# A gated-delta layer with 32 experts on one core: input in groups, other places, other loads and another order of the work

## The chip, the core and the metric

The kernel runs on one core of a Trainium2 chip. The core has five engines that run side by side and meet only at semaphores: TensorE (PE: matmuls and transposes, into eight banks of PSUM), VectorE (DVE), ScalarE (ACT), GpSimd (POOL) and SyncE (SP), whose queue issues nearly all DMAs here. The metric is the device time of one execution in microseconds (us). Each engine works through its own instructions in the order in which the program lists them; an instruction that waits holds up all behind it. A DMA is issued by a queue and lands later.

## What is computed

For x of 2048 tokens by 256 features, all in fp32:

```python
x = x + attn(layernorm(x))
x = x + ffn(layernorm(x))

# attn
qkv = silu(causal_conv4(x @ W_qkv.T))         # 2048 channels
z, beta = x @ W_z.T, sigmoid(x @ W_b.T)
g = -exp(A_log) * softplus(x @ W_a.T + dt_bias)
q, k = l2norm(q) * 64 ** -0.5, l2norm(k)      # 8 heads of 64, each for 2 of 16 value heads
# per token t and head: S = S*exp(g_t); S += k_t (v_t - k_t S)^T * beta_t; o_t = q_t S
y = norm_weight * rmsnorm(o) * silu(z)
return y @ W_out.T

# ffn
h = rmsnorm(x) * norm_w
w, ids = top_k(softmax(h @ router_w.T), 4)    # 32 experts, w normed to sum 1
routed = sum_k w_k * ((silu(h @ w1_g) * (h @ w1_u)) @ w2)[ids_k]
return x + routed + (silu(h @ sg) * (h @ su)) @ sd
```

## The kernel before

**Work.** The recurrence is done by chunks of 64 tokens: 32 chunks, four in a pair of blocks; a block has 128 tokens, so there are 16 blocks and 8 pairs `p`. For each pair a *front* does what does not need the state: `proj p s i` (PE, eight slices `s` of two tiles), `mul` (ACT) and `tap` (DVE), `sum` (POOL) and `silu` for the convolution, `ss`, `ssq`, `rpow` for the norms, `kt`, `kn`, `kb`, `ke` to bring k into shape, `scan p c` for the decay between tokens of chunk `c`, `kk` and `nt` for the products within a chunk, and then the inverse of a unit triangular matrix for 32 heads and chunks at once: `lg`, `lx`, 31 steps of elimination `el` on DVE (lines 829 and 832), `xt` (its second transpose is line 896), `ta`, `pm`, `pe`, `tm`, `tc`. A *chain* goes through the chunks with the state: `kqs`, `ktb`, `v`, `ks`, `qs`, `r`, `sd`, `u`, `ue`, `ku`, `au`, `su`, `oe`; `su n` adds to the state and ends chunk `n`. A *tail* finishes each block: `osq`, `nin`, `npow`, `yn`, `yt`, `yg`, `op` (output product), `x2`, `xn`, `hh` (norms), `ht`, `htb`, `rt` (router), `mx`, `ex`, `tk`, `rank`, `slot` (top 4 and the places of the rows), and `send`, four indirect DMAs of POOL that write the rows to DRAM, sorted by expert.

**Experts.** After that come 16 shared items (one for each block) and 95 tiles of 128 sorted rows. Step `n` of `experts` does the up product of item `n`, the transposes of item `n-1` and the down product of item `n-2`. The rows of a tile go to DRAM (`picked`), and at the end each block's four rows are loaded, summed and stored.

**Order.** One list, `SCHEDULE`, is walked by every engine; each takes from it the stages that it has a part in. It is made by sorting the stages of all pairs by a planned time, `PAIR * p + t`, with `t` from tables of numbers that are the same for every pair. `banks_in_turn` gives the short-lived results one of four PSUM banks in turn.

**SP's part.** SP walks the same list. `dload p` loads the decay tables of the four chunks of pair `p + 1`, two DMAs for each chunk, each after `nt` has freed its place; `scan` waits for them. `ebload n` loads the decay of chunk `n + 1`, `xload p` the columns of pair `p + 1`, `xin` the rows of a block. `base b` stores `base` and, after a wait for `htb`, the transposed rows of block `b`. `blanks b` writes 4.2 MB of blank rows to DRAM (`blank_ranks`), which `send` needs two blocks later. `early` loads the first half of the expert weights (6.7 MB, with the two shared experts) over the front's places after the last `tc`; after the last chunk SP loads the other half and the results of 15 blocks.

**Opening.** Before the list, the whole x is normed in a few large operations, transposed, multiplied for the gates, and the tables are made and stored. The first `proj` follows.

Of the kernel before, what the change touches and what calls it, by code (L numbers as in the profile page):

```python
# [9 lines left out]
ALU = mybir.AluOpType  # L10
X = mybir.AxisListType.X

P = 128
# [28 lines left out]
TURNS = 4  # L42

# [3 lines left out]
PAIR = 95.20  # L47
FRONT = [(-89.34, "nd", 0), (-88.1, "nd", 1), (-60.93, "proj", 0, 0), (-59.88, "proj", 0, 1), (-59.83, "xload"), (-59.78, "blank"),
    (-58.65, "mul", 0, 0), (-57.71, "mul", 0, 1), (-56.59, "tap", 0), (-54.5, "proj", 1, 0), (-54.49, "sum", 0), (-53.45, "proj", 1, 1),
    (-53.16, "silu", 0), (-51.88, "mul", 1, 0), (-51.7, "proj", 2, 0), (-50.94, "mul", 1, 1), (-50.65, "proj", 2, 1),  # L50
    (-49.42, "mul", 2, 0), (-49.38, "tap", 1), (-48.48, "mul", 2, 1), (-47.3, "sum", 1), (-45.97, "silu", 1), (-44.51, "proj", 3, 0),
    (-43.46, "proj", 3, 1), (-42.53, "tap", 2), (-42.23, "mul", 3, 0), (-41.29, "mul", 3, 1), (-40.45, "sum", 2), (-38.31, "ss", 0),
    (-36.67, "tap", 3), (-36.13, "silu", 2), (-34.59, "sum", 3), (-33.91, "ssq", 0), (-33.44, "rpow", 0), (-33.26, "silu", 3),
    (-31.8, "ss", 1), (-29.8, "kt", 0), (-28.65, "kt", 1), (-28.47, "kn", 0), (-27.5, "kb", 0), (-26.27, "ke", 0), (-25.35, "kn", 1),
    (-20.49, "ssq", 1), (-20.11, "kb", 1), (-20.11, "rpow", 1), (-18.88, "ke", 1), (-18.61, "proj", 4, 0), (-17.56, "proj", 4, 1),
    (-16.33, "mul", 4, 0), (-15.39, "mul", 4, 1), (-10.62, "tap", 4), (-8.72, "scan", 0), (-7.49, "sum", 4), (-5.84, "silu", 4),
    (-5.29, "nd", 2), (-4.84, "proj", 5, 0), (-3.79, "proj", 5, 1), (-3.16, "scan", 1), (-2.56, "mul", 5, 0), (-1.74, "nd", 3),
    (-1.62, "mul", 5, 1), (-1.29, "kk", 0), (0.09, "tap", 5), (2.69, "nt", 0), (4.44, "scan", 2), (4.47, "sum", 5), (5.68, "scan", 3),
    (5.8, "silu", 5), (5.87, "proj", 6, 0), (6.92, "proj", 6, 1), (8.84, "mul", 6, 0), (9.78, "mul", 6, 1), (10.9, "tap", 6),
# [30 lines left out]
def schedule():  # L90
# [7 lines left out]
    for _, item in sorted(timed, key=lambda e: e[0]):  # L98
        out.append(item)
        if item[1] == NB - 1 and item[0] in ("x2", "xn", "rt", "ex", "tk", "rank", "slot", "send") and step < NB - 3:  # L100
            out.append(("experts", step))
            step += 1
# [1276 lines left out]
```

## Time and profile before

| | |
|---|---|
| three runs, median (lowest to highest) | 1275.51 us (1269.92 to 1276.7) |
| profiled execution: its own time | 1274.97 us |
| its span, first to last instruction | 1273.2 us |
| mean granted TensorE clock | 0.839 of full |
| busy: PE, DVE, POOL, ACT | 978.7, 822.4, 557.4, 530.0 us |
| moved by DMA | 165.67 MB, mean 130 GB/s |

The span is that of the profiled execution; the few us between it and the execution's time lie around the first and the last instruction. A busy time is the sum of an engine's instructions over the span; which engine sets the pace in a stage must be read from that stage. The granted clock is a mean; PE's instructions have two lengths, one for each of its two clocks.

### The profile page before, as it was taken

The page shows a single profiled execution, that of the slowest core. Times are in us where ns is not written, and L with a number is a line of the kernel's source. Part 1 is how long each engine was busy: PE and PEld are TensorE (multiplying, and loading weights), DVE is VectorE, ACT ScalarE, POOL GpSimd, SP SyncE. Part 2 cuts the span into 40 slices and gives each one's busy share as a digit, 9 for nine tenths or more (in the row PEclk, how much of TensorE's full clock was granted, in tenths as well). Part 3 has the DMA queues.
Part 4 walks back from the last instruction along what each step waited for, and adds up shares of the span by engine and source line. Part 5 has one row for each costly group of instructions (what it writes and reads, how often), then busy time and mean ns, then how long its engine had stood idle before and what let it go on. Part 6 is the DMA issues. An engine that isn't in the chain of part 4 may idle for free.

```text
span 1273.2 us, 32965 instructions
## 1 busy us (share of the span) xinstructions
PE 978.7 (77%) x12871; PEld 819.2 (64%) x12871; DVE 822.4 (65%) x1859; ACT 530.0 (42%) x1042; POOL 557.4 (44%) x507
## 2 busy tenths in 40 slices
PE   0685599789889879978977986886785799989940
PEld 0573577667778677767867776775674467767730
DVE  5227867877896986888689698779333343333345
ACT  1343365256355544625635453451332224434410
POOL 2034454465364555546445554543342105545530
PEclk9768689769779976977987897697697999999975
DMA  5373302055326706714640670661796814444346
GB/s 213 75 193 95 96 11 60 23 149 149 89 63 155 182 23 164 190 39 114 160 124 21 169 200 23 160 169 34 178 350 250 276 42 126 128 123 130 110 144 204
DMA packets 182359, 165.67 MB, mean 130 GB/s; under 512 B 75699, under 2 KB 174908, under 8 KB 181312
## 3 DMA queue, kind: packets, MB, share of 16 engines
q1 hardware_dynamic: 172272, 144.60, 41.3%
q0 software_dynamic: 7632, 16.87, 4.2%
q8 instruction: 106, 1.74, 0.6%
q10 hardware_dynamic: 2304, 2.10, 0.5%
q14 instruction: 45, 0.37, 0.1%
HBM read 66.03 MB, written 101.55 MB: 132 GB/s over the span
## 4 chain that ended last, share of the span: by engine, by line
PE 38%; DVE 33%; issue 11%; POOL 7%; DMA 7%; ACT 3%; SPq 1%; DVEq 0%; POOLq 0%; ACTq 0%
DVE arena L829 6%; DVE arena L832 6%; PE ps L1305 6%; PE ps L1093 4%; POOL nrm L503 3%; DVE arena L845 3%; PE ps L1156 3%; PE ps L1238 3%; PE ps L1102 2%; PE ps L1328 2%; DMA out<-work 2%; POOL slotted L580 2%; DVE work L920 2%; DMA work<-htd 2%; PE ps L1296 2%
## 5 line engine op out<-in xcount | busy, mean ns | idle before, releaser
L1093 PE MATMUL ps<-work,arena 128*128 128x259 f32 x512 | 164.0, 475 | 18.8 <-DVE arena L845 16.3
L531 POOL TENSOR_TENSOR arena<-arena 128x512 f32<-128x512 f32 x64 | 84.7, 1324 | 141.6 <-DVE arena L845 141.5
L1093 PEld LDWEIGHTS ps<-work,arena 128*128 128x128 f32 x512 | 116.3, 238 | 45.6 <-DVE arena L845 18.8
L591 POOL DMA_INDIRECT picked<-work x95 | 93.4, 983 | 113.0 <-DVE work L1026 64.2
L845 DVE SCALAR_TENSOR_TENSOR arena<-ps,cw,arena 128x256 f32<-128x256 f32 x256 | 107.1, 475 | 55.3 <-ACT arena L640 55.2
L1016 DVE TENSOR_TENSOR work<-work,ps 128x128 f32<-128x128 f32 (+1 forms) x111 | 34.0, 307 | 139.7 <-ACT work L746 113.2
L832 DVE TENSOR_TENSOR arena<-arena 128x31 f32<-128x31 f32 (+15 forms) x248 | 117.8, 475 | 8.5
L829 DVE TENSOR_TENSOR arena<-arena 128x31 f32<-128x31 f32 (+15 forms) x248 | 104.1, 420 | 7.5 <-POOL arena L511 1.3
L1305 PE MATMUL ps<-arena,work 128*128 x380 | 102.0, 391 | 7.1 <-issue 6.2
L646 ACT ACTIVATE arena<-arena 128x512 f32<-128x512 f32 x64 | 40.3, 629 | 157.6 <-POOL arena L531 157.6
L580 POOL DMA_INDIRECT slotted<-hr,slots x64 | 65.1, 1016 | 79.8 <-DVE slots L983 65.2
L1173 PE MATMUL ps<-work 64*64 64x64 f32 x1024 | 46.1, 253 | 54.6 <-DVE work L901 54.6
L746 ACT ACTIVATE work<-ps 128x128 f32<-128x128 f32 (+1 forms) x111 | 32.5, 292 | 119.7 <-PE ps L1305 56.0
L1173 PEld LDWEIGHTS ps<-work 64*64 64x64 f32 x1024 | 42.1, 165 | 57.8 <-issue 57.7
L1305 PEld LDWEIGHTS ps<-arena,work 128*128 128x128 f32 x380 | 65.3, 191 | 19.7 <-issue 14.2
L524 POOL TENSOR_TENSOR work<-work,nbeta 128x512 f32<-128x512 f32 x32 | 43.9, 1383 | 69.0 <-DVE ndb L810 50.5
L553 POOL TENSOR_TENSOR work<-arena,work 128x512 f32<-128x512 f32 x64 | 73.5, 1168 | 0.0
L1238 PE MATMUL ps<-work 128*128 128x256 f32 x256 | 66.7, 419 | 8.6 <-DVE work L926 7.4
L639 ACT ACTIVATE arena<-ps,cw 128x256 f32<-128x256 f32 x128 | 60.6, 474 | 23.9 <-PE ps L1093 16.8
L1238 PEld LDWEIGHTS ps<-work 128*128 128x128 f32 x256 | 54.2, 214 | 20.5 <-DVE work L926 10.4
L503 POOL TENSOR_TENSOR small<-small,mhalf 128x1 f32<-128x1 f32 x32 | 18.4, 576 | 98.6 <-DVE small L944 59.3
L1222 PE MATMUL ps<-work 128*128 128x256 f32 x256 | 61.0, 387 | 0.3 <-ACT work L715 0.2
(223 smaller groups left out, 2328.2 us busy)
## 6 DMA issues: line engine op xcount, KB each, us to landing
slotted<-blank SPq DMA_DIRECT2D x17, 4128.0 KB, 20.1
arena<-in_w SPq DMA_DIRECT2D x2, 6528.0 KB, 18.6
work<-slotted SPq DMA_DIRECT2D x95, 129.0 KB
arena<-tab SPq DMA_DIRECT2D x64, 128.0 KB, 3.4
work<-tab SPq DMA_DIRECT2D x64, 128.0 KB, 3.3
arena<-picked SPq DMA_DIRECT2D x16, 512.0 KB, 4.8
work<-xtd SPq DMA_DIRECT2D x8, 259.0 KB, 10.5
arena<-in_x SPq DMA_DIRECT2D x1, 2048.0 KB, 8.5
```

The lines of the kernel that those rows point to most:

```text
L531: g.tensor_tensor(ca[:, f % 2, :, :], ca[:, f % 2, :, :], conv_to(p, s_), ALU.add).then_inc(S["sum_out"], 1)
L553: g.tensor_tensor(kqs[:, n % 2, kind, :, :].rearrange("p (kt r) t -> p kt r t", r=2), kqn[:, p % 2, kind, :, lo:lo + C].unsqueeze(2).broad ...
L580: g.indirect_dma_start(out=slotted, out_offset=bass.IndirectOffsetOnAxis(ap=slots[:, k:k + 1], axis=0), in_=hr[:, k, :], in_offset=None).t ...
L591: g.indirect_dma_start(out=picked, out_offset=bass.IndirectOffsetOnAxis(ap=to, axis=0), in_=yrow[:, j % SLOTS, :], in_offset=None, bounds_ ...
L829: v.tensor_tensor(t, nl[:, j + 1:H, j:j + 1].broadcast_to([P, rows, cols]), tl[:, j:j + 1, 0:cols].broadcast_to([P, rows, cols]), ALU.mult ...
L832: v.tensor_tensor(tl[:, j + 1:H, 0:cols], tl[:, j + 1:H, 0:cols], t, ALU.add).then_inc(S["el"], 1)
L845: v.scalar_tensor_tensor(out=acc_, in0=bank_of("proj", p, s_, i)[:, k:k + W2], scalar=cw[:, u, k:k + 1], in1=acc_, op0=ALU.mult, op1=ALU.a ...
L1093: ins = mm(to[:, 0:WX], wqkv[:, k, m:m + P], xt2[:, p % 3, k, :], start=k == 0, stop=k == KD - 1)
L1173: ins = mm(KS[half(hp), DH * h:DH * h + DH], kqs[half(hp), n % 2, 0, h, :], state[half(hp), h, :], start=False, stop=h == KR - 1)
L1222: ins = mm(to[:, W2 * j:W2 * j + W2], wz[:, d, m:m + P], xt2[:, p % 3, d, TAPS - 1:TAPS - 1 + W2], start=d == 0, stop=d == KD - 1)
L1238: ins = mm(W3[:, 0:DIM], ygt[:, u, :], wo[:, u, :], start=u == 0, stop=u == UT - 1)
L1305: ins = mm(up_[:, 0:2 * I], ht[:, j % 2, k, :], arena[:, bass.ds(at_ + 2 * I * k, 2 * I)], start=k == 0, stop=k == KD - 1)
```

## The change

- **x in groups.** x is loaded in three groups of 2, 6 and 8 blocks, with the weights of the projections between the first and the second. Each group is normed by itself: `bn_stats` and `bn_aggr` on DVE, the small steps for 1/sqrt, and one scaled copy for each block on ACT, in place. The first transposed columns are copied straight into the first pair's place as well, and the first four projections are done at once; the gate products and the tables are cut into steps (`gate 0` to `gate 3`, `tables`) that stand in the list among the first pair's stages.
- **Decay loads per chunk.** `dload p c` loads the table of chunk `c` of pair `p` itself, and stands in the list by itself; `scan p c` is done during pair `p - 1`.
- **New order.** New tables of planned times: one for pairs 0 to 5, one for pair 6, one for pair 7. A few items are put behind what they need (`HELD`).
- **Late loads.** `late` stands in the list behind the last of `base 13` and `ebload 30`. It waits for the end of the chain, loads the results of 12 blocks and then the second part of the expert weights. `early` keeps its place behind the last `tc`. The results of the other four blocks are loaded after the last `base`.
- **Shared experts in the last tails.** Up to 12 of their steps stand behind stages of the last two blocks, once the chain and `slot 13` have gone by.
- **Final sums.** Each block has its own place for its four rows, is summed in place and stored from there; eight loads may be in flight, and the sums no longer wait for stores.
- PE's waits move to where the data is needed, and `sd` also waits for `ks`.

SP's items of one pair (from the last `xt` of pair 3 on), by the old list and by the new one, without those in which SP has nothing to do:

```text
before: ebload 14, blanks 4, xin 5, base 5, ebload 15, dload 4 (pair 5, all four chunks), blanks 5, xload 5
after:  ebload 14, xin 5, dload 5 0, base 5, dload 5 1, ebload 15, dload 5 2, blanks 5, dload 5 3, xload 5
```

DVE's items from the transposes of pair 3 to the next `lx`, by the new list:

```text
xt 3, tap 4 4, x2 5, tap 4 5, xn 5, nt 4 0, nt 4 1, hh 5, scan 5 0, scan 5 1, tap 4 6, mx 5, su 12, tk 5,
nt 4 2, slot 5, su 13, scan 5 2, nt 4 3, nin 6, tap 4 7, scan 5 3, yn 6, lx 4
```

PE's: `pm 3, kk 4 0, kk 4 1, tm 3, proj 4 6, u 12, ht 5, z 3 0, rt 5, ku 12, au 12, kk 4 2, ks 13, ...`. In the last pair SP has: `xin 13, base 13, late, early, blanks 13, xin 14, base 14, blanks 14, base 15`.

The core of the diff:

```diff
+GROUPS = ((0, 2), (2, NB // 2), (NB // 2, NB)) if NB > 4 else ((0, 2), (2, NB))
+SOON = max(NB - 4, 1)
-PAIR = 95.20
+PAIR = 97.66
+STEADY = {
...
+    "dload": [(-77.6, 0), (-74.8, 1), (-59.4, 2), (-53.3, 3)],
+    "scan": [(-74.7, 0), (-71.9, 1), (-56.4, 2), (-49.4, 3)],
...
+    "kk": [(16.9, 0), (17.9, 1), (33.2, 2), (40.9, 3)],
+    "nt": [(18.1, 0), (19.8, 1), (36.3, 2), (42.5, 3)],
...
+    "blanks": [(190.7, 0), (236.2, 1)],
+}
+def opening():
+    out = [("norm", 0), ("turnx", 0)] + [("proj", 0, s, i) for s in range(2) for i in range(2)]
+    for g in range(1, len(GROUPS)):
+        out += [("norm", g), ("turnx", g)]
+        if g == 1:
+            out += [("mul", 0, s, i) for s in range(2) for i in range(2)]
+    return out + [(name, 0, s) for s in range(2) for name in ("tap", "sum", "silu")] + [("gate", 0)]
+GATES = [(("tap", 0, 2), [("gate", 1)]),
+         (("tap", 0, 3), [("gate", 2), ("gate", 3), ("tables", 0)] + [("dload", 0, c) for c in range(4)] + [("ebload", -1)]),
...
+HELD = {item: cause for c in range(4) for item, cause in (
+    (("dload", 1, c), ("nt", 0, c)), (("scan", 1, c), ("dload", 1, c)), (("nd", 1, c), ("scan", 1, c - 2))) if cause[2] >= 0}
...
+        if item in ready:
+            ready.remove(item)
+            if not ready:
+                out.append(("late", 0))
+        if item == ("tc", NP - 1):
+            out.append(("early", 0))
+        if not before and item[0] in FILL and item[1] >= NB - 2 and step < SOON:
...
-                if name == "dload" and ix[0] + 1 < NP:
-                    for n in range(4 * (ix[0] + 1), 4 * (ix[0] + 1) + 4):
-                        wait(sp, S["at_out"], n - 3)
+                if name == "dload":
+                    p, c = ix
+                    n = 4 * p + c
+                    wait(sp, S["at_out"], n - 3)
...
-                if name == "oe" and ix[0] == NC - 1:
+                if name == "late":
                     sp.wait_ge(S["au_mm"], NC)
                     sp.wait_ge(S["s_out"], NC)
+                    load_results(0, 0, SOON)
                     load_experts(1)
-                    load_results(0, 0, NB - 1)
...
+            def norm(g):
+                lo, hi = GROUPS[g]
+                n = hi - lo
+                shift, var, rstd, t0, t1 = (small[:, k, lo:hi] for k in range(5))
...
+                dve.wait_ge(s_x0[g], 16)
+                for k in range(n):
+                    ins = v.bn_stats(stats[:, k, :], xall[:, lo + k, :])
+                done(ins)
+                for k in range(n):
+                    ins = v.bn_aggr(both[:, k, :], stats[:, k, :])
+                done(ins)
...
-                wait(dve, s_o[b % 2], 16 * (b // 2))
-                v.tensor_tensor(frow[:, b % 2, :], two[:, 0, :], acc[:, b, :], ALU.add).then_inc(S["fin_out"], 1)
+                v.tensor_tensor(four[:, 0, :], four[:, 0, :], acc[:, b, :], ALU.add).then_inc(S["fin_out"], 1)
```

## Rows read from the trace of the kernel before

**Rows 1.** The page, part 4: the chain that ended last, by engine.

```profile
PE 38%; DVE 33%; issue 11%; POOL 7%; DMA 7%; ACT 3%; SPq 1%; DVEq 0%; POOLq 0%; ACTq 0%
```

**Rows 2.** Windows by stage: length; busy of PE, PEld, DVE, ACT, POOL; clock; DMA share; GB/s.

```profile
469.00:577.30 108.30, 92.94 (x1451) 80.56 (x1450) 87.40 (x195) 54.35 (x92) 56.61 (x46) 0.82 0.47 119
792.00:889.40 97.40, 74.14 (x1148) 64.13 (x1148) 77.66 (x175) 39.31 (x59) 42.76 (x38) 0.79 0.45 119
889.40:967.50 78.10, 59.93 (x1044) 52.38 (x1044) 30.94 (x88) 28.29 (x41) 28.28 (x25) 0.82 0.73 223
967.50:1042.50 75.00, 56.64 (x198) 34.65 (x199) 27.86 (x100) 15.79 (x39) 11.88 (x11) 0.86 0.69 234
1227.70:1273.20 45.50, 0.00 (x0) 0.00 (x0) 23.32 (x48) 0.00 (x0) 0.00 (x0) 0.50 0.73 231
```

**Rows 3.** Waits of DVE in one pair: total, times, longest; first and last of nine.

```profile
DVE arena L845 <- ACT arena L640: 4.2, 2, 3.3
...
DVE arena L885 <- issue: 0.6, 1, 0.6
```

**Rows 4.** Timeline of the opening, DVE and PE: start, us, what, idle before.

```profile
10.11 4.42 DVE L779 TENSOR_REDUCE small<-arena 128x16 f32<-128x4096 f32 x1 [10.11 <-DMA arena<-in_a_log]
...
41.56 5.77 PE L1056 MATMUL ps<-arena 128*64 128x16 f32 x191 [0.79 <-ACT arena L608]
49.24 3.17 PE L1056 MATMUL ps<-arena 128*64 128x16 f32 x65 [1.91 <-issue]
...
63.43 1.20 PE L1093 MATMUL ps<-work,arena 128*128 128x259 f32 x2 [0.95 <-ACT arena L624]
```

**Rows 5.** Timeline of ACT and PE in the stretch after the transposes, of two pairs.

```profile
579.18 2.07 ACT L677 ACTIVATE work<-arena,kbm 128x1024 f32<-128x1024 f32 x1 [1.64 <-DVE arena L896]
581.26 3.95 ACT L680 ACTIVATE work<-arena 32x1024 f32<-32x1024 f32 x2
...
490.46 1.41 PE L1156 MATMUL ps<-arena 32*32 32x32 f32 x43
...
492.88 2.58 PE L1156 MATMUL ps<-arena 32*32 32x32 f32 x84 [0.49 <-issue]
```

**Rows 6.** SP's issues in a pair; landings: L364, L383 there; L383, L394, L388 in all.

```profile
523.51 0.62 SPq L364 DMA_DIRECT2D slotted<-blank  x1
527.73 8.17 SPq L383 DMA_DIRECT2D work<-xtd  x1
...
DMA to landing us min/median/max: 20.5/20.5/20.5
...
DMA to landing us min/median/max: 17.4/17.4/17.4
...
DMA to landing us min/median/max: 4.0/16.5/18.1
...
DMA to landing us min/median/max: 3.0/3.3/5.0
...
DMA to landing us min/median/max: 2.9/3.4/4.4
```

**Rows 7.** SP's issues of the two parts of the expert weights.

```profile
916.12 0.35 SPq L425 DMA_DIRECT2D arena<-in_w  x1
...
967.50 0.33 SPq L425 DMA_DIRECT2D arena<-in_w  x1
```

**Rows 8.** Timeline of PE: the first shared expert, and two steps of later ones.

```profile
991.77 5.40 PE L1296 MATMUL ps<-arena,work 128*128 128x512 f32 x8 [5.06 <-DMA work<-htd]
...
1033.70 1.88 PE L1296 MATMUL ps<-arena,work 128*128 128x512 f32 x4
...
1036.50 1.88 PE L1296 MATMUL ps<-arena,work 128*128 128x512 f32 x4
```

**Rows 9.** Timeline of the final sums: their loads, and DVE's first.

```profile
1227.74 35.13 SPq L450 DMA_DIRECT2D arena<-picked  x16
...
1231.65 0.69 DVE L1035 TENSOR_TENSOR work<-arena 128x512 f32<-128x512 f32 x1 [7.90 <-DMA arena<-picked]
```

More of the change, by code:

```diff
@@ new lines @@
+ENDING = [END_0, END_1]
+PER_CHUNK = ("kqs", "ebload", "ktb", "v", "ks", "qs", "r", "sd", "u", "up", "ue", "ku", "su", "au", "oe")
+PER_BLOCK = ("osq", "nin", "npow", "yn", "yt", "yg", "op", "x2", "xin", "lnp", "xn", "rmp", "hh", "base", "hr", "ht", "htb", "rt", "mx", "ex",
+             "tk", "rank", "slot", "send", "blanks")
+FILL = ("nin", "yn", "op", "x2", "xn", "hh", "rt", "mx", "tk", "rank", "slot")
+def opening():
[5 more added lines that the diff above has]
+    return out + [(name, 0, s) for s in range(2) for name in ("tap", "sum", "silu")] + [("gate", 0)]
@@ L90, in schedule @@
 def schedule():
[L91 removed]
+    timed = []
     for p in range(NP):
[L93 to L100 removed]
+        table = STEADY if p < NP - len(ENDING) else ENDING[p - NP]
+        for name, times in table.items():
+            for t, *ix in times:
+                if name in PER_CHUNK:
+                    ix[0] += 4 * p
+                elif name in PER_BLOCK:
+                    ix[0] += 2 * p
+                else:
+                    ix = [p, *ix]
+                timed.append((PAIR * p + t, (name, *ix)))
@@ new lines, in schedule @@
+    out, step, before, ready = [], 0, {("oe", NC - 1), ("su", NC - 1), ("slot", NB - 3)}, {("base", NB - 3), ("ebload", NC - 2)}
+    planned = [item for _, item in sorted(timed, key=lambda e: e[0])]
+    head = opening()
+    moved, gates = set(head).union(*(then for _, then in GATES)), list(GATES)
+    first = head + [item for item in planned if item not in moved]
+    for item, cause in HELD.items():
+        if item in first and first.index(item) < first.index(cause):
+            first.remove(item)
+            first.insert(first.index(cause) + 1, item)
@@ L101, in schedule @@
+    for item in first:
+        out.append(item)
+        while gates and gates[0][0] in out:
+            out += gates.pop(0)[1]
+        before.discard(item)
+        if item in ready:
[5 more added lines that the diff above has]
+        if not before and item[0] in FILL and item[1] >= NB - 2 and step < SOON:
             out.append(("experts", step))
@@ L141, in banks_in_turn @@
             taken += 1
-    return out
-TURN = banks_in_turn()
+    return out, last
+TURN, LAST = banks_in_turn()
 class Chain:
@@ L628, in stage @@
+            def stage(name, *ix):
+                if name == "norm":
+                    norm(*ix)
+                if name == "turnx":
+                    transposed(*ix)
+                if name == "gate":
+                    gate(*ix)
                 if name == "mul":
@@ L1179, in stage @@
                     wait(pe, S["o_out"], n)
+                    wait(pe, S["s_out"], n)
                     for h in range(KR):
```

458 lines of the change are left out of this document (306 added, 152 removed), and 110 rows, old and new, of tables (CHAIN, END_0, END_1, FRONT).

## The prediction

> **What bounds the kernel now.** The page comes first: no engine is full, and the chain that ended last changes hands between PE (38%) and DVE (33%) [rows 1]. Such a share says nothing of a stage, so the span is cut at the eight transposes of line 896, one for each pair of blocks, and at the ends of the chain of chunks, of the shared experts and of the tiles [rows 2]. The first elimination starts at 123.2 us. Then come pairs of about 107.6 us each; in the one shown DVE is busy 87.4 of 108.3 us and PE 92.9. The last pair but one takes 97.4 us, the stage to the end of the chain 78.1 us, the shared experts with the last tail 75.0 us, and the final sums 45.5 us.
>
> The waits of DVE in that pair are short: nine groups, 4.2 us the largest, 17.8 us in all [rows 3]. So 90.5 us of the pair are DVE's own work and the gaps between its instructions, and each wait added in its queue lengthens the pair, unless another shrinks. None of the nine is for a load: this is what I expect to change.
>
> **The opening.** Before, DVE starts when 2 MB of x and the small inputs are in, at 10.1 us, and the transposes at 34.6; the gate products take from 41.6 to 52.4, and the first projection starts at 63.4 [rows 4]. After, the first 256 KB should be in at about 4 us (an eighth of the load that is in at 10.1 us). Two blocks need two statistics of the kind that `x2` takes (0.4 us each), the two aggregations and 14 small steps of about 0.2, so 4.2 us; the scaled copies, four transposes and two copies 3 us: first projection at about 11 us, not 63.4. The other two groups keep DVE until about 28 us and the last transposed columns leave at about 34. There PE does the gate products, 10.9 us, to 45. Slices 2 and 3 and the gate steps, with the queues waiting on each other, run to 58. The blanking of 4.2 MB, issued at about 44, now stands ahead of the decay table on SP's queue; as such a write takes about 20 us [rows 6], the table is stored at 64, its four loads issue in 5.4 us and land at 73, and the scans end at 75. Slices 4 to 7 took 28 us from there before; they keep this length, since the four scans that leave them make room for four new ones with short waits for loads of 3.4 us [rows 6]. First elimination: 103 us. **-20 us**, between -25 (the waits for pair 1's loads are covered) and -12 (each costs 4 us in full). The removed work (two passes of 4.4 us over x on DVE, ACT's square, the two stores of zeros) is in this difference.
>
> **The pairs.** The work is the same; the order and the loads are not. SP is in order, and two of its items stand in the way of the decay loads, on which DVE's scans wait.
>
> First, `dload q 1` stands behind `base`, which waits until `htb` of the same block is out. From the end of the transposes `xt` to that `htb`: `ta` 6.0 us, `pe` 1.1, `tm` 4.9 (490.5 to 495.4) [rows 5], `tc` 2.4, `u` 1.1, `ht` and `htb` 0.8, together 16.3 (`pe`, `tc`, `u`, `ht` and `htb` by their lengths in the same stretch); then 0.4 for the store's issue, 0.6 for the first half's and 3.4 to the landing of the second: 20.8 us. DVE's own work over that stretch is two `tap` (3.3), `x2` (1.3), `xn` (0.8), two `nt` (3.4), `hh` (1.9) and one scan (1.3), 12.0 us. New wait, that of the first scan included: about 9 us. At least 5, if the matmuls and `tc` run side by side; 10 at most. Queued behind that scan are `tap` 6, `su` and `tk`, and PE's `ks` waits for `su`.
>
> Second, `dload q 3` stands right behind `blanks`, a write of 4.2 MB. The trace has this very arrangement with another load: the write issued at 523.5 took 20.5 us, and the load of xt issued at 527.7 was held 8.2 us in issue and landed 17.4 us after it began, at 545.1, one us after the write; a decay load with nothing in front lands in 3.4 [rows 6]. In the new order `blanks` issues 1.3 us after the third `nt` of the pair, so the fourth load lands some 23 us after that `nt`. DVE has until then `slot` (1.8), `su` (0.7), the third scan (1.3), the fourth `nt` (1.7), `nin` (1.8) and `tap` 7 (1.6): 8.9 us. New wait: 14 us, the third scan's included; 12 if the write takes 18 us, 16 if 22. Behind the fourth scan stand `yn`, `lx` and the whole elimination of the next pair.
>
> The Trainium skill (DMA: Bandwidth & Descriptors, "Anatomy of one DMA") fits a DMA of its GpSimd path as 2.0 us plus its bytes at 436 GB/s, which gives 11.7 us for this write. By the 20.5 us of the row the new wait is 14 us, by the page about 5, and the whole forecast would be 1264 us. The row has the very write, so the sum goes by it.
>
> So a pair has 90.5 us of work, 24 us of new waits and what is left of the old ones. While DVE is held, the other engines catch up, and the old waits (for `op`, `ss`, `kt`, `yt`, `ex`) should fall from 17.8 to about 5: 119.5 us, 11 to 12 more than now. If the old waits vanish and the first stall is the small one, it is 6 more; if 10 us of them stay, 16. The loads of pairs 3 to 7 stand so, five stretches between transposes: **+56 us**, between +30 and +80. Pair 2's loads have neither item ahead of them and cost nothing new. In the stretch of 97.4 us there are no decay loads any more, and the four scans have gone an interval earlier: **-5 us**, between 0 and -9.
>
> **The last pair.** After the last transposes the new order has only `x2` to `slot` of block 13 ahead, where the old one had block 13's norm and products too, and the four chunks follow each other at about 10 us. From `xt`: `pm` 3.9, two `z` 4.0, `tm` 4, `z` and `tc` 3, `u`/`ku`/`su` of chunk 28 at 18, `su` 29 at 26, `su` 30 at 37 (it stands behind `yn` 14), `su` 31 at 50 to 54. With the 1.9 us of the transpose the stage is 55 us, not 78.1: **-23 us**, between -14 and -28.
>
> But `late` stands ahead of `early` in SP's queue, and waits for the end of the chain. Before, the first 6.7 MB of expert weights were issued at 916.1, and only the second part and the results at 967.5 [rows 7]; the results landed 24.2 us later, 8.65 MB at 357 GB/s, and PE started at 991.8 [rows 8]. After, the results of 12 blocks (3.1 MB) and both parts of the weights, the one that the shared experts need last, go out then: 16.5 MB, 46 us at that rate. PE's first shared expert waits for it, and PE's queue holds behind it `ht` and `rt` of block 14 and all that is left of block 15. From there: 16 experts of 2.8 us (44.8), 2.6 for the slow first, 8.2 of tails on PE, and 7.5 between `rt` 15 and `rank` 15, which no expert covers now. 109 us instead of 75.0: **+34 us**, between +24 (the load at 400 GB/s, the tail covered) and +38.
>
> **The tiles** keep their order and loads: 0. **The final sums** no longer wait for the stores of two blocks before. The stretch moves 10.5 MB in 45.5 us with the DMA engines busy 0.73 of it [rows 2]; full, that is 33 us, while DVE needs 16 x 1.55 = 25, which is hidden; with 3.8 us until the first block is there [rows 9], 37 us. **-8 us**, between -3 and -12.
>
> **Sum.** -20 + 56 - 5 - 23 + 34 - 8 = +34. The profiled execution took 1275.0 us (span 1273.2), the median of the runs 1275.5, so the base is the same: 1309 us. A measurement of this kernel can tell about 0.5%, 6.4 us, from no change.
>
> **Rivals.** (a) *The fourth load does not wait for the blanking.* A later load's packets may pass, or the blanking may be over sooner. For it: no load of `ebload` took more than 5.0 us to land, though a write is in flight for 20 of every 50 us. Against: of the seven xt loads, of which five stand close behind a write, the median is 16.5 us and the longest 18.1 [rows 6]. The fourth scan's wait falls from 14 to about 3 and 55 us go: 1254 us, faster. It decides as soon as that load lands within 12 us of the third `nt`. Chance 0.11. (b) *The new order fits better than I read it.* All old waits vanish, the `base` stall is the small one, +6 a pair: 1282 us, and with the opening or the weights at their good ends, within the noise. Chance 0.14. (c) *Nothing is caught up.* 10 us of old waits stay, +16 a pair: 1333 us. Chance 0.13. (d) *The weights arrive in time*: if SP's three loads share the engines and the shared experts start at 25 us after the chain, 21 us less: 1288 us. Against it is that the results behind 6.7 MB came last before. Chance 0.07. (e) *The forecast*, its own range 1288 to 1326: 0.55.
>
> **Numbers.** Faster: (a) and a little of (b), 0.13. Within 0.5%: the good ends of (b), 0.08. Slower: 0.79. Range for 8 in 10: 1268 to 1338, which leaves out most of (a) and the far end of (c).
>
> **What would show it.** In the changed kernel's profile: the first projection at 11 us, the first elimination at 103; transposes `xt` some 119 us apart from the second to the sixth interval; DVE's scan, which waits for nothing now, with waits on the decay load of about 9 and 12 us in each pair; PE idle some 46 us before the first shared expert, on the weights; out stores with no DVE wait on them. I am wrong if the scans' waits are a few us, or if the transposes stay 107 us apart with the waits elsewhere.

## The result, and the profile after

| | median (lowest to highest) | |
|---|---|---|
| before, on the same chip | 1275.4 us (1269.92 to 1276.7) | 4 runs |
| after | 1337.6 us (1333.2 to 1339.46) | 4 runs |
| ratio | 1.0491, interval 1.045 to 1.0532 | slower by 62 us |

The profiled execution of after took 1338.96 us, its span is 1337.2. The forecast was 1309 us: the sign, the two stalls in a pair and the late weights came as expected, the size did not. Part 4 of the page after, the chain that ended last, by engine and by line:

```profile
PE 41%; DVE 20%; issue 14%; DMA 12%; SPq 5%; POOL 4%; ACT 3%; another core or an unknown queue 0%; POOLq 0%; DVEq 0%; ACTq 0%
DMA arena<-tab 7%; PE ps L1398 5%; PE ps L1616 5%; DVE arena L1113 5%; PE ps L1549 4%; DVE arena L1116 4%; SPq L638 3%; DVE arena L1134 3%; PE ps L1452 2%; PE ps L1462 2%; PE ps L1408 2%; PE ps L1511 2%; PE ps L1442 2%; PE ps L1607 2%; PE ps L1639 2%
```

DVE had 33% of that chain [rows 1] and has 20. The largest share of a single line is now the load of the decay tables (`arena<-tab`, 7%, and 3% for its issue on L638), which is not among the 15 largest lines of that chain before. The windows of after, cut as [rows 2]; the second transpose is line 1185 now:

```profile
148.10:252.10 104.00, 85.43 (x1424) 74.47 (x1425) 78.87 (x164) 49.37 (x82) 49.84 (x40) 0.85 0.29 74
...
496.60:624.40 127.80, 97.08 (x1452) 83.57 (x1451) 85.64 (x195) 53.50 (x88) 55.63 (x46) 0.80 0.39 101
...
964.30:1017.60 53.30, 51.14 (x942) 44.06 (x940) 19.37 (x49) 24.33 (x32) 16.82 (x16) 0.87 0.06 20
1017.60:1126.00 108.40, 56.11 (x204) 34.06 (x205) 29.68 (x108) 20.13 (x46) 12.44 (x12) 0.78 0.77 261
...
1307.00:1337.20 30.20, 0.00 (x0) 0.00 (x0) 23.32 (x48) 0.00 (x0) 0.00 (x0) 0.50 0.90 347
```

One pair takes 127.8 us and not 108.3 [rows 2], with nearly the same number of instructions on every engine (ACT has 88 and not 92); the five between the second transposes and the seventh take 619.4 instead of 537.9. By stage, from the two traces:

| stage | before | after | difference | forecast |
|---|---|---|---|---|
| start to the first elimination | 123.2 | 104.7 | -18.5 | -20 |
| to the first second transpose | 40.8 | 43.4 | +2.6 | 0 |
| first to second | 90.1 | 104.0 | **+13.9** | 0 |
| second to seventh, five pairs | 537.9 | 619.4 | **+81.5** | +56 |
| seventh to eighth | 97.4 | 92.8 | -4.6 | -5 |
| to the end of the chain of chunks | 78.1 | 53.3 | -24.8 | -23 |
| to the first tile | 75.0 | 108.4 | +33.4 | +34 |
| tiles | 185.2 | 181.0 | -4.2 | 0 |
| final sums | 45.5 | 30.2 | -15.3 | -8 |
| sum | 1273.2 | 1337.2 | +64.0 | +34 |

**Where a pair loses its time.** The timeline of DVE in the pair from 496.6, the two transposes and the four scans, with the idle time before each and its releaser:

```profile
496.64 1.89 DVE L1185 STREAM_TRANSPOSE arena<-arena 128x1024 f32<-128x1024 f32 x1
...
512.61 1.23 DVE L1156 TENSOR_TENSOR_SCAN arena<-arena,work 128x512 f32<-128x512 f32 x1 [2.30 <-DMA arena<-tab]
...
521.00 1.23 DVE L1156 TENSOR_TENSOR_SCAN arena<-arena,work 128x512 f32<-128x512 f32 x1 [7.16 <-DMA arena<-tab]
...
541.35 1.23 DVE L1156 TENSOR_TENSOR_SCAN arena<-arena,work 128x512 f32<-128x512 f32 x1 [5.46 <-DMA arena<-tab]
...
559.81 1.23 DVE L1156 TENSOR_TENSOR_SCAN arena<-arena,work 128x512 f32<-128x512 f32 x1 [12.62 <-DMA arena<-tab]
```

And SP's issues in the same pair:

```profile
508.16 1.93 SPq L638 DMA_DIRECT2D arena<-tab  x2
510.34 0.42 SPq L653 DMA_DIRECT2D base<-row  x1
516.62 0.38 SPq L655 DMA_DIRECT2D htd<-htb  x1
517.05 1.26 SPq L638 DMA_DIRECT2D arena<-tab  x2
533.98 2.33 SPq L644 DMA_DIRECT2D work<-tab  x2
536.36 1.35 SPq L638 DMA_DIRECT2D arena<-tab  x2
537.75 0.62 SPq L610 DMA_DIRECT2D slotted<-blank  x1
544.03 7.09 SPq L638 DMA_DIRECT2D arena<-tab  x2
```

The reader sees both stalls as they were forecast. From 510.8 to 516.6 SP stands at `base`, waiting for `htb`; only then does the second load go out (517.05), and the second scan starts at 521.0. The fourth load is held for 7.1 us in issue behind the blank write and is there only when DVE's scan starts, at 559.8, 22 us after that write was issued. In the five pairs the four scans wait 2.2, 7.3, 4.6 and 12.5 us on average. That is 9.4 us for the first stall, where the forecast had 9, and 17.1 for the second, where it had 14; the difference is mostly in the third scan, whose load goes out behind `ebload` (533.98). Over the whole kernel, the waits of DVE on the scans' loads, by the view of its waits (total us, times, longest), and the landing times of the loads, counted from the start of their issue:

```profile
DVE arena L1156 <- DMA arena<-tab: 148.7, 30, 12.9
```

```profile
DMA to landing us min/median/max: 2.8/3.2/14.5
```

**The other stages.** PE's first instructions, SP's queue at the end of the chain, PE's first shared expert, and the final sums:

```profile
11.23 4.97 PE L1398 MATMUL ps<-work,arena 128*128 128x259 f32 x12 [1.27 <-ACT arena L868]
...
1017.58 0.37 SPq L680 DMA_DIRECT2D work<-htd  x1
...
1018.51 4.37 SPq L675 DMA_DIRECT2D arena<-in_w  x2
...
1023.41 43.96 SPq L649 DMA_DIRECT2D xin<-in_x  x1
...
1060.05 5.34 PE L1607 MATMUL ps<-arena,work 128*128 128x512 f32 x8 [42.65 <-issue]
...
1306.79 16.39 SPq L700 DMA_DIRECT2D arena<-picked  x16
```

The first projection starts at 11.2 us (63.4 in [rows 4]). Both parts of the weights go out 0.9 us behind the end of the chain, where in [rows 7] the first part went out 51.4 us ahead of it, and PE stands 42.7 us. The releaser of that wait reads "issue", so the view does not name the weights; that they are the cause is shown by the run below with `early` ahead of `late`.

### The profile page after: what moved, and what is told of

Its sections match the earlier page's. It is cut to its first block, busy times and chain, and to the rows that moved or that the text cites. A ratio compares the mean times of both kernels' runs of the same rounds, so it can differ in the third digit from the quotient of the medians.

```text
span 1337.2 us, 33264 instructions
## 1 busy us (share of the span) xinstructions
PE 993.3 (74%) x12871; PEld 825.6 (62%) x12871; DVE 810.1 (61%) x1915; ACT 541.3 (40%) x1063; POOL 542.7 (41%) x507
## 2 busy tenths in 40 slices
DMA packets 181833, 165.41 MB, mean 124 GB/s; under 512 B 75428, under 2 KB 174125, under 8 KB 180785
## 4 chain that ended last, share of the span: by engine, by line
PE 41%; DVE 20%; issue 14%; DMA 12%; SPq 5%; POOL 4%; ACT 3%; another core or an unknown queue 0%; POOLq 0%; DVEq 0%; ACTq 0%
DMA arena<-tab 7%; PE ps L1398 5%; PE ps L1616 5%; DVE arena L1113 5%; PE ps L1549 4%; DVE arena L1116 4%; SPq L638 3%; DVE arena L1134 3%; PE ps L1452 2%; PE ps L1462 2%; PE ps L1408 2%; PE ps L1511 2%; PE ps L1442 2%; PE ps L1607 2%; PE ps L1639 2%
## 5 line engine op out<-in xcount | busy, mean ns | idle before, releaser
L1398 PE MATMUL ps<-work,arena 128*128 128x259 f32 x512 | 173.0, 494 | 24.6 <-DVE arena L1134 17.6
L1398 PEld LDWEIGHTS ps<-work,arena 128*128 128x128 f32 x512 | 121.1, 249 | 58.0 <-DVE arena L1134 24.6
L781 POOL TENSOR_TENSOR arena<-arena 128x512 f32<-128x512 f32 x64 | 83.6, 1309 | 164.2 <-DVE arena L1134 164.1
L1156 DVE TENSOR_TENSOR_SCAN arena<-arena,work 128x512 f32<-128x512 f32 x32 | 40.7, 1274 | 153.2 <-DMA arena<-tab 148.7
L1116 DVE TENSOR_TENSOR arena<-arena 128x31 f32<-128x31 f32 (+15 forms) x248 | 123.3, 497 | 8.5
L1113 DVE TENSOR_TENSOR arena<-arena 128x31 f32<-128x31 f32 (+15 forms) x248 | 119.2, 481 | 7.1 <-POOL arena L761 1.3
L1134 DVE SCALAR_TENSOR_TENSOR arena<-ps,cw,arena 128x256 f32<-128x256 f32 x256 | 105.8, 475 | 15.2 <-ACT arena L913 15.2
L1542 PE MATMUL ps<-ident,work 128*128 128x128 f32 x128 | 26.6, 345 | 96.1 <-DVE work L1215 55.4
L753 POOL TENSOR_TENSOR nrm<-nrm,mhalf 128x16 f32<-128x16 f32 x16 | 46.8, 2927 | 88.1 <-DVE nrm L1200 88.1
L1542 PEld LDWEIGHTS ps<-ident,work 128*128 128x128 f32 x128 | 18.2, 174 | 103.5 <-issue 60.7
L1532 PE MATMUL ps<-work 128*128 128x256 f32 x256 | 66.4, 406 | 16.3 <-DVE arena L1168 15.6
L1549 PE MATMUL ps<-work 128*128 128x256 f32 x256 | 72.1, 444 | 8.0 <-DVE work L1215 8.0
L774 POOL TENSOR_TENSOR work<-work,nbeta 128x512 f32<-128x512 f32 x32 | 35.5, 1111 | 101.5 <-DVE arena L1156 101.0
L803 POOL TENSOR_TENSOR work<-arena,work 128x512 f32<-128x512 f32 x64 | 70.1, 1115 | 0.0
```

Source lines behind the costliest of these rows:

```text
L781: g.tensor_tensor(ca[:, f % 2, :, :], ca[:, f % 2, :, :], conv_to(p, s_), ALU.add).then_inc(S["sum_out"], 1)
L803: g.tensor_tensor(kqs[:, n % 2, kind, :, :].rearrange("p (kt r) t -> p kt r t", r=2), kqn[:, p % 2, kind, :, lo:lo + C].unsqueeze(2).broad ...
L1113: v.tensor_tensor(t, nl[:, j + 1:H, j:j + 1].broadcast_to([P, rows, cols]), tl[:, j:j + 1, 0:cols].broadcast_to([P, rows, cols]), ALU.mult ...
L1116: v.tensor_tensor(tl[:, j + 1:H, 0:cols], tl[:, j + 1:H, 0:cols], t, ALU.add).then_inc(S["el"], 1)
L1134: v.scalar_tensor_tensor(out=acc_, in0=bank_of("proj", p, s_, i)[:, k:k + W2], scalar=cw[:, u, k:k + 1], in1=acc_, op0=ALU.mult, op1=ALU.a ...
L1398: ins = mm(to[:, 0:WX], wqkv[:, k, m:m + P], xt2[:, p % 3, k, :], start=k == 0, stop=k == KD - 1)
```

## The experiments

Ratios are against the kernel before on the chip of that run. These were two other chips, on which before took 1263.3 to 1265.0 us (medians). A ratio of 0.01 is 12.75 us on the scale of the first table, and "against after" is the difference to 1.0491 so converted.

The kernel after was not run on those chips, and the conversion makes the gains somewhat too small. Before is 10 us faster there, but the parts of after that an experiment leaves alone are not: the five pairs take 621.0 us in the run with only `early` moved and 619.4 in the table above, and from the issue of the first results to the end it is 319.6 us in after and in both runs that move one item of the pairs. Put together from these traces (964.0 us to the eighth transpose, 370.4 from there), after would have a span of about 1334 us on the chip of the first four runs. This is an estimate; where it matters, the difference of the spans is given as well.

### Both pair terms, each undone alone and together

The blank writes of the odd blocks go behind `xload` (the order of before had them behind all four decay loads too, but ahead of `xload`):

```diff
+    for q in range(3, NP):
+        item, cause = ("blanks", 2 * (q - 3) + 1), ("xload", q)
+        if first.index(item) < first.index(cause):
+            first.remove(item)
+            first.insert(first.index(cause) + 1, item)
```

> The changed kernel, with the write of blank rows that stands ahead of each pair's fourth decay load put behind the load of xt that follows it (pairs 3 to 7); nothing else moves. Theory (the queue stalls): the fourth scan waited 12 to 13 us for its load; with no write ahead the load lands 3 to 4 us after the fourth nt, so the wait falls to about 2 us and each of the five intervals from 252 to 871 us gets 10 us shorter: 1287 us, between 1280 and 1297. Rival (other waits take over: the order itself, with PE, holds a pair near 120 us): the scan's wait falls but DVE waits for PE instead, 3 us or less a pair, 1323 us or more.

Measured: 1282.48 us (1280.12 to 1285.5), ratio 1.0125, interval 1.0092 to 1.0157: -47 us against after (-51 by the spans, 1283.8 against 1334). The scans' waits for loads fall from 148.7 to 93.8 us. The write ahead of the fourth load costs what the theory said.

The same five lines with `("base", 2 * (q - 3) + 1)` behind `("dload", q, 1)`:

> The changed kernel, with the item base of the odd blocks put behind the second decay load instead of ahead of it (pairs 3 to 7), so that SP does not wait for htb first. Theory (the queue stalls): the second scan's wait falls from 7.2 us to at most 1, five times: 1307 us, between 1302 and 1316. Rival (what follows the scan waits for PE's tm, u and ks anyway, as the next su does): the wait moves to mx and su, and the time stays within 7 us of 1338.

Measured: 1291.84 us (1289.56 to 1294.96), ratio 1.0206, interval 1.0169 to 1.0243: -36 us against after (-44 by the spans). The waits fall to 114.6 us.

Both:

> Both moves together. Theory: the two stalls lie one behind the other in DVE's queue and add up: 10 and 6 us a pair, 80 us in all, 1257 us, between 1247 and 1272; pairs of about 108 us. Rival: gains overlap, or PE takes over: pairs of 113 us or more, 1280 us or more.

Measured: 1245.62 us (1241.27 to 1249.16), ratio 0.9849, interval 0.9813 to 0.9885: -82 us against after (-95 by the spans), and 1.5% under before. The two add up (47 + 36, or 51 + 44). The five pairs of this run in the view of windows; then the five pairs of the run on the kernel before that changes only the final sums (below), where before takes the same time; and one pair's waits of DVE for its loads in this run (15.3 us with all others):

```profile
251.50:780.80 529.30, 443.87 (x7221) 386.01 (x7221) 439.14 (x967) 268.06 (x440) 271.98 (x228) 0.87 0.46 121
```

```profile
254.00:783.00 529.00, 447.83 (x7222) 391.52 (x7221) 438.99 (x967) 267.35 (x442) 283.78 (x230) 0.85 0.45 121
```

```profile
DVE arena L1166 <- DMA arena<-tab: 8.3, 4, 5.3
```

The five pairs of all these runs, from the traces, in us; work and gaps are the time less both kinds of waits:

| | five pairs | DVE waits on decay loads | its other waits | work and gaps |
|---|---|---|---|---|
| before | 537.9 | 0 | 85.3 | 452.6 |
| after | 619.4 | 132.7 | 46.3 | 440.4 |
| only `early` moved (below): pairs as in after | 621.0 | 132.4 | 41.8 | 446.8 |
| blank writes behind | 569.5 | 73.7 | 42.0 | 453.8 |
| `base` behind | 579.2 | 95.2 | 35.3 | 448.7 |
| both | 529.3 | 40.4 | 33.6 | 455.3 |
| pairs as in before, only the final sums changed | 528.9 | 0 | 74.1 | 454.8 |

So the loss of the five pairs, 92 us on that chip (621.0 to 529.3), hangs on two places in SP's queue. With both undone the new order makes pairs of 105.9 us on average, and the old one makes pairs of 105.8 where before takes as long. Its own gain in the pairs is nothing that these runs can tell: it gives back 40 us of other waits and has 40 us of waits on loads for them.

### The weights: early ahead of late

```diff
-    ... {("base", NB - 3), ("ebload", NC - 2)}
+    ... {("base", NB - 3), ("ebload", NC - 2), ("tc", NP - 1)}
+        if item == ("tc", NP - 1):
+            out.append(("early", 0))
         if item in ready:
             ready.remove(item)
             if not ready:
                 out.append(("late", 0))
-        if item == ("tc", NP - 1):
-            out.append(("early", 0))
```

> The changed kernel, with early (first half of the expert weights) ahead of late in SP's queue and all else as it is. Theory (weights late): after the chain only the results, 3.1 MB, are waited for, some 5 us for their first half, so the first shared expert starts some 5 us after the chain instead of 42, and 33 to 38 us go: 1302 us, between 1297 and 1308. Rival (the tails of blocks 14 and 15, which now run among the experts with nothing done in advance, or the loads behind, set the time): less than 20 us go, 1318 us or more.

Measured: 1308.31 us (1304.19 to 1311.77), ratio 1.0332, interval 1.0291 to 1.0374: -20 us against after (-28 by the spans, of which 26 lie between the issue of the first results and the end: 293.6 us and not 319.6), less than the theory's -33 to -38. SP and PE of this run:

```profile
982.09 0.40 SPq L675 DMA_DIRECT2D arena<-in_w  x1
...
1014.23 3.73 SPq L675 DMA_DIRECT2D arena<-in_w  x1
1018.00 0.53 SPq L610 DMA_DIRECT2D slotted<-blank  x1
1018.57 29.94 SPq L649 DMA_DIRECT2D xin<-in_x  x1
...
1057.78 0.39 SPq L610 DMA_DIRECT2D slotted<-blank  x1
...
1074.73 0.36 SPq L680 DMA_DIRECT2D work<-htd  x1
```

```profile
1020.17 5.74 PE L1607 MATMUL ps<-arena,work 128*128 128x512 f32 x8 [7.06 <-DMA work<-htd]
...
1079.66 3.75 PE L1607 MATMUL ps<-arena,work 128*128 128x512 f32 x4 [8.87 <-DMA work<-htd]
```

The wait before the first shared expert falls from 42.7 to 7.1 us, so the mechanism is right. But 10 to 16 of the 36 us are given back at once: the rows of block 15 (`xin`) are held for 29.9 us in issue behind the second part of the weights and a blank write, and the results of the last blocks go out at 1074.7 behind a second blank write, for which PE waits another 8.9 us. What is late next is SP's queue itself.

All three moves together:

> The changed kernel with all three moves: blanks of the odd blocks behind xload, base of the odd blocks behind the second decay load, early ahead of late. Theory (the terms are independent, each a place in SP's queue): the two moves of the pairs gave -82 us, early first gave -20, so ratio to the kernel before 0.969 (0.96 to 0.98). Rival (with the pairs shorter, early is issued closer to the blank write of block 12 and gives back part): 0.98 or more.

Measured: 1224.24 us (1223.21 to 1228.72), ratio 0.9705, interval 0.9667 to 0.9743: -100 us against after, the sum of -82 and -20 within its interval.

### Does the fourth load wait for the queue or for the DMA engines?

Only the fourth decay load of pairs 3 to 7 is issued from ScalarE's queue. The blank write stays where the new order has it, on SP's.

```diff
-                if name == "dload":
+                if name == "dload" and (ix[1] < 3 or ix[0] < 3):
...
+                if name == "dload" and ix[1] == 3 and ix[0] >= 3:
+                    n = 4 * ix[0] + 3
+                    act.wait_ge(S["tab_stored"], 16)
+                    wait(act, S["at_out"], n - 3)
+                    for hp in range(2):
+                        act.dma_start(decay[half(hp), 3, :, :], tab[0, n * KR:(n + 1) * KR, half(hp)].unsqueeze(0).broadcast_to(
+                            [C, KR, C])).then_inc(s_d[3], 16)
```

> The changed kernel with the fourth decay load of pairs 3 to 7 issued by ScalarE's queue at the same place in the list; the blank write and all else stay. Theory (the load waits because it stands behind the write in the same queue): the load lands some 4 us after its issue while the write is in flight, the fourth scan's wait of 12.6 us goes, as with the blank write moved: -45 us against the changed kernel, ratio 1.013. Rival (the 4.2 MB keep the 16 DMA engines busy, whatever queue issues the load): the load lands with the write, the wait stays, ratio 1.04 to 1.05. ScalarE's wait for nt and two issues cost it some 2 us a pair, which it has.

Measured: 1315.73 us (1313.53 to 1324.37), ratio 1.044, interval 1.0389 to 1.0492. Against after that is -6.5 us by the ratios, whose intervals overlap, and some -22 by the spans (1311.8 against about 1334, the estimate above, which is for the other of the two chips; before takes the same time on both). In the traces the five pairs take 602.7 us, against 621.0 in the run with `early` moved, whose pairs are those of after: -18, where moving the write gave -51. So the rival was right for about two thirds, and the queue has the rest. The write, ACT's issue of the load behind it, DVE's scan, the waits in all, and the landing times of the ten loads on ACT's queue:

```profile
528.24 0.66 SPq L610 DMA_DIRECT2D slotted<-blank  x1
...
533.75 2.02 ACTq L899 DMA_DIRECT2D arena<-tab  x2
...
546.16 1.23 DVE L1163 TENSOR_TENSOR_SCAN arena<-arena,work 128x512 f32<-128x512 f32 x1 [8.07 <-DMA arena<-tab]
```

```profile
DVE arena L1163 <- DMA arena<-tab: 126.8, 28, 8.1
```

```profile
DMA to landing us min/median/max: 8.7/10.1/11.8
```

From the write's issue to that scan, the window has the DMA engines full (their busy share reads 1.07):

```profile
528.30:546.10 17.80, 12.28 (x147) 9.88 (x145) 5.87 (x11) 9.30 (x17) 6.84 (x5) 1.00 1.07 293
```

No such load is held in issue now, and none lands in the 3.2 us of an unhindered one: with the write in flight it takes 8.7 to 11.8 us, on another queue too. So of the fourth scan's wait of 12.6 us about 4.5 went with the queue; the 8 that stay go with the full DMA engines. The Trainium skill (DMA: Bandwidth & Descriptors, "Queues, rings and completion order") says that each DMA engine takes packets in turn from the queues that have work for it. The trace agrees as far as it goes: the load on its own queue is there 17.9 us after the write was issued, when no such write in the kernel before was over in less than 18.0 us (median 20.1), and it is late all the same. The landing of this write is not in the trace, so that the two took turns is not shown by itself. What helps is a load issued *before* the write, as in the first experiment.

### Single parts alone, on the kernel before

The final sums: 16 places instead of four, the sum in place, the store from there, eight loads in flight.

```diff
-                wait(sp, S["fin_out"], b - 3)
-                sp.dma_start(fin4[:, b % 4, :, :], rows[b]).then_inc(s_f[b % 4], 16)
+                wait(sp, S["fin_out"], b - 7)
+                sp.dma_start(fin[:, b, :, :], rows[b]).then_inc(s_f[b % 8], 16)
...
-                wait(dve, s_o[b % 2], 16 * (b // 2))
-                v.tensor_tensor(frow[:, b % 2, :], two[:, 0, :], acc[:, b, :], ALU.add).then_inc(S["fin_out"], 1)
+                v.tensor_tensor(four[:, 0, :], four[:, 0, :], acc[:, b, :], ALU.add).then_inc(S["fin_out"], 1)
```

> The kernel before with one part of the change alone: 16 places for the final rows, summed in place and stored from there, eight loads in flight. Theory (the stretch was held by the loads' and stores' latencies; with the places it is set by the 10.5 MB at about 350 GB/s): -15 us as between the two traces, ratio 0.988. Rival (my forecast's term, with its 37 us): -8 us, 0.9935. Second rival (the gain in the changed kernel came from its earlier stages): no change, 1.0.

Measured: 1249.91 us (1247.63 to 1252.35), ratio 0.989, interval 0.9853 to 0.9928: -14 us, the theory's value; my -8 lies just outside the interval. The loads' issues, in 16.3 us where [rows 9] had 35.1:

```profile
1219.80 16.34 SPq L450 DMA_DIRECT2D arena<-picked  x16
```

Then the results of 15 blocks ahead of the second part of the weights:

```diff
-                    load_experts(1)
                     load_results(0, 0, NB - 1)
+                    load_experts(1)
```

> The kernel before, with the results of 15 blocks loaded ahead of the second part of the expert weights instead of behind it. Theory (the first shared expert waits for the results, which stand behind 6.7 MB): the results land 10 us after their issue instead of 24, the wait of 5.1 us goes, and the experts go into PE's idle stretches of the last tail: -5 us, ratio 0.996, at most 0.992. Rival (the tail of block 15 and the tile rows set the end of this stretch, and the weights and the blank write behind come as late as before): no change, 1.0.

Measured: 1264.71 us (1259.99 to 1271.66), ratio 1.001, interval 0.9989 to 1.003: no change. PE's wait of 5.1 us before the first shared expert [rows 8] is gone, and this row has come in its place:

```profile
986.85 0.69 PE L1246 MATMUL ps<-ident,hr 128*128 128x128 f32 x2 [8.18 <-DVE hr L950]
```

The first expert now runs ahead of the tail of the last block, and then PE waits for that tail. In before the results were not what set the end of this stage.

### Where the last tail's loads belong

From the run with all three moves: `ebload` behind the third decay load, blank write 13 ahead of `xin 13`, and blank write 14 and the second part of the weights behind the last `base` and the last results.

```diff
+        item, cause = ("ebload", 4 * (q - 2) + 3), ("dload", q, 2)
...
+    for item, cause, at in ((("blanks", NB - 3), ("xin", NB - 3), 0), (("blanks", NB - 2), ("base", NB - 1), 1)):
+        first.remove(item)
+        first.insert(first.index(cause) + at, item)
...
                     if b == NB - 1:
                         load_results(1, SOON, NB)
+                        load_experts(1)
```

> The kernel with all three moves, and in addition: ebload behind the third decay load; the blank write 13 ahead of xin 13, where SP's queue is idle; the blank write 14 and the second part of the expert weights behind base 15 and the last results. Theory: in the run with early first alone, xin 14 was held 30 us in issue behind the second part of the weights and the last results stood behind the blank write 14, and PE waited 8.9 us for them; with these behind, the last tail and its experts go on and 10 to 15 us go; the third scan's wait of 4.6 us in a pair falls to about 2, five times 2.5 = 12 us. Ratio 0.949 to 0.955. Rival (the last tail is set by its own chain of operations, and the third scan by nt just ahead of its load): no more than 5 us, ratio 0.965 or more.

Measured: 1222.05 us (1213.38 to 1223.53), ratio 0.9653, interval 0.9605 to 0.9701. That is 2 us less than with the three moves by the medians and 7 by the ratios, and the intervals overlap: the rival's number. But not for its reason. The part of the theory on the third scan came, and more: the five pairs take 510.2 us and not 528.1, and DVE's waits on the decay loads in them fall from 38.5 to 20.3 us (the third scan's, in one pair, from 5.6 to 0.7). So `ebload` ahead of the third load was a third place in SP's queue, worth 18 us. The other part cost as much as this gave: from the issue of the first results to the end it is 313.0 us and not 293.7, as SP and PE of this run show:

```profile
962.20 0.37 SPq L698 DMA_DIRECT2D work<-htd  x1
...
963.13 0.50 SPq L693 DMA_DIRECT2D arena<-in_w  x1
963.67 0.43 SPq L628 DMA_DIRECT2D slotted<-blank  x1
1000.28 100.05 SPq L710 DMA_DIRECT2D work<-slotted  x53
```

```profile
1002.37 0.69 PE L1612 MATMUL ps<-ident,work 128*128 128x128 f32 x2 [25.28 <-DMA work<-slotted]
```

The last results go out at 962 instead of 989; then the first tile's rows stand behind the two transfers that I had put last, and PE waits 25.3 us. The last try puts the blank write 14 directly behind `early`, where SP has nothing to do for 35 us, and the second part of the weights directly behind `base 14`. Against the run before it:

```diff
-            out.append(("early", 0))
+            out += [("early", 0), ("blanks", NB - 2)]
...
                     if b == NB - 1:
                         load_results(1, SOON, NB)
-                        load_experts(1)
+                    if b == NB - 2:
+                        load_experts(1)
```

> The kernel with all moves of e6_loads_placed, but the blank write 14 directly behind early, where SP's queue is idle for 35 us, and the second part of the expert weights directly behind base 14. Theory (in e6_loads_placed the last results went out 27 us sooner than in e5_all_three, at 962 instead of 989, but PE then stood 25.3 us before the first tile, whose rows came behind that part of the weights and that blank write, at 1000): now these two are over at about 945 and the first tile's rows go out at about 970, so 20 us go: ratio 0.950 (0.945 to 0.957). Rival (the stretch before the first tile is set by the last block's rank, places, sends and table, and not by the two transfers): the rows go out at 990 or later, ratio 0.96 or more.

Measured: 1190.5 us (1184.45 to 1197.36), ratio 0.9401, interval 0.9372 to 0.9429: better than the theory's 0.945 to 0.957, the best of all, 6% under before and 139 us under after. SP at the end of the chain:

```profile
872.04 0.40 SPq L694 DMA_DIRECT2D arena<-in_w  x1
872.48 0.45 SPq L628 DMA_DIRECT2D slotted<-blank  x1
907.43 0.37 SPq L699 DMA_DIRECT2D work<-htd  x1
...
923.27 0.47 SPq L694 DMA_DIRECT2D arena<-in_w  x1
...
974.63 25.70 SPq L711 DMA_DIRECT2D work<-slotted  x15
```

The first tile's rows go out at 974.6, 26 us sooner than in the run before it. The same bytes are moved as in after (165.41 MB). Against the run with the three moves, 21 of the 26 us of span come from the five pairs (506.8 and not 528.1), that is, mostly from the place of `ebload`, and the rest from the end. DVE's waits on decay loads are not gone: 17.7 us are left in the five pairs.

## Why the prediction was right in direction and too small

- **The opening, -20: right** (-18.5; first projection 11.2 us, forecast 11; first elimination 104.7, forecast 103).
- **The interval from the first transposes to the second, taken as 0: wrong, +13.9.** The forecast costed the new order only from pair 3 on. In this window DVE is busy 78.9 us with 164 instructions, before 68.4 with 135. The two lists say what has come in: `mx`, `tk` and `slot` of block 0, `su 3`, `nin`, `yn` and `yg` of block 1 and `r 4` stood behind the next transposes and stand ahead of them now. This work is not new; it is given back at the end, where DVE is busy 19.4 us in the last stage and not 30.9 [rows 2], within the -24.8 of that stage, a forecast that was read from the new list by itself. So I took the gain of an order that runs further ahead and left out its price in the first interval. The rest is waits, 22.5 us and not 19.5. Among them the scans wait 9.2 us for the tables of pair 2, which are loaded in this interval; the prediction said of these loads that they cost nothing new. No experiment undid this by itself; it is read from the lists and the trace.
- **The five pairs, +56: the failed step, mis-sized; +81.5.** The two stalls were placed rightly and nearly rightly sized: forecast 24 us a pair, measured 26.5 (132.7 in five). That they are the cause of the loss is shown: undone, the five pairs are 92 us shorter. What failed is "the old waits should fall from 17.8 to about 5". The other waits of DVE are 9.3 us a pair on average (11.4 in the pair shown), 46.3 in the five pairs. The two largest groups there:

```profile
DVE work L1190 <- PE ps L1511: 14.8, 10, 2.3
DVE cnt L1267 <- PE ps L1571: 11.0, 6, 2.6
```

The old waits did fall: of the kinds that before had, 19.8 us are left, 4.0 a pair (the first row, `su`, has even grown from 7.0 us). But 26.5 us, 5.3 a pair, are waits at places where DVE waited for nothing in these pairs before: `slot` for `rank` (the second row), `nt` for `kk`, `hh` for the norm's power, `mx` for `rt`. The sum has no term for waits that the new order brings outside the loads. With both stalls undone 20.7 us of them are still there, so they go with the order more than with the stalls. By the pair the miss is +2.5 in the stalls, +4.3 in the other waits, -2.4 in work and gaps (88.1 us against 90.5), and +0.7 since the five pairs of before average 107.6 us and the sum was built on the one of 108.3: together 5.1, and 25.5 in five.

I had argued that the other engines catch up while DVE is held. PE did not: in the five pairs, for the same matmuls (7222 and 7228 records), it was busy 466.9 us at a granted clock of 0.81, before 454.6 at 0.83; with the stalls undone 443.9 at 0.87, on the other chip. The clock and the waits move together in these runs; which of them leads, no experiment here separates. The average of rival (c), +16 a pair, is what came (16.3), and its 10 us of waits too (9.3), but more than half of these are not old ones.

- **Seventh to eighth, -5: right** (-4.6). **The last pair, -23: right** (-24.8).
- **The late weights, +34: right** (+33.4), with PE's wait of 42.7 us for the forecast 46. The experiment showed the mechanism, and that undoing it alone gives back only 20 to 28 us of it.
- **The tiles, 0:** -4.2; not looked into. **Final sums, -8: mis-sized, -15.3.** The term took 33 us of full DMA engines for the bytes (0.73 of 45.5) and added 3.8 until the first block is there. The stretch took 30.2 us with the engines busy 0.90 of it, that is 27 us of full engines for the same bytes. So the busy share of before was no measure of what the bytes need; why it is less now is not shown.
- **The rivals.** (a) did not come: the fourth scan waited 12.0 to 12.9 us in each of the five pairs. By the Trainium skill's fit for its GpSimd path (DMA: Bandwidth & Descriptors, "Anatomy of one DMA") this write would take 11.7 us, an estimate; the fourth load was there 22 us after the write's issue, so the 20.5 us of [rows 6] were the better guide. (b) did not come (+16 a pair and not +6), nor (d) (the first shared expert started 42.5 us after the chain and not 25).

The sum of the misses: +25.5 in the pairs, +13.9 and +2.6 before them, -7.3 and -4.2 at the end, and -0.5 in the other four stages together: +30, from +34 to +64.

## What to carry to other kernels

A load that some engine waits for must be issued before a large transfer, not merely on another queue; so list, for each in-order DMA queue, what stands ahead of every awaited load, including the waits of the items there, and put the large transfers where that queue is idle. When an order is moved, cost every interval from the list, the first and the last too: what runs earlier at the end was paid for earlier. And look in the new list for places where an engine will wait that did not wait before: here they were 5 us a pair, in a sum that looked only at the old waits and the loads. Where runs come from several chips, compare stages in the traces as well as ratios.

## What the hardware showed that was not expected

- A load of 128 KB that lands in 3.2 us takes 8.7 to 11.8 us while a write of 4.2 MB is in flight, though it is alone on ScalarE's queue; in SP's queue behind that write it takes up to 14.5 us from the start of its issue, and the issue itself up to 7.2 of these.
- PE's granted clock falls in the runs in which DVE waits more: over the five pairs it is 0.81 with 179 us of waits on DVE, 0.83 in before with 85, and 0.87 with 74 when both stalls are undone, for the same matmuls (7221 to 7228 records); PE's busy time is 466.9, 454.6 and 443.9 us. That the stall is what lowers it, and not the other way round, is argued and not shown by itself, and the last run is from another chip.
- DVE's own busy time in the five pairs moves the other way: 424.2 us in after, 430.5 with the same pairs on the other chip, 439.1 with the stalls undone, for 966 or 967 instructions. Why is not shown.
